# Relative attention with a routed expert gate: left sums by GpSimd in the window's first column, a block transpose on VectorE at a head's end, a slot table laid out by rows, output weights loaded early

## Chip, cores and metric

The kernel runs on one core of one Trainium2 chip. The metric is the device time of one execution in microseconds (us), median of several runs. A core has five engines that each work through their own instructions in order: TensorE (PE in the rows, with its weight loads as PEld), VectorE (DVE), ScalarE (ACT), GpSimd (POOL) and SyncE (SP, which here only issues DMAs). They wait for each other through semaphores.

## The reference

```python
xn = layernorm(x)                                  # x: (2, 2048, 256), f32
q, k, v = proj(Wq, bq), proj(Wk, bk), proj(Wv, bv)  # 16 heads of 16
idx = clip(arange(S)[None, :] - arange(S)[:, None], -128, 128) + 128
content  = einsum('bhqd,bhkd->bhqk', q, k)
relative = einsum('bhqd,qkd->bhqk', q, rel_k[idx])
w = softmax((content + relative) / sqrt(16))
s = (einsum('bhqk,bhkd->bhqd', w, v) + einsum('bhqk,qkd->bhqd', w, rel_v[idx])) @ Wo.T + bo
y = (gelu(xn @ W1[e]) @ W2[e])   # for each token the expert e = argmax(xn @ Wg + bg), 8 experts
x + s * silu(y)
```

The relative values `rel_v[idx]` are constant for all keys more than 128 to the left (`rel_v[0]`) and more than 128 to the right (`rel_v[256]`). Only in a window of 256 relative positions round the diagonal do they differ from key to key.

## The kernel before

It has three stages, each a block of its own with a barrier between: `project` (layernorm, q, k, v, gate logits, and the table arithmetic that gives every token a slot of its expert), `attend` (32 pairs of head and batch, called heads here), and `experts` (output projection, then 39 tiles of 128 slots through the experts).

`attend` is one software pipeline written out by hand. A head has 16 steps, one for each block of 128 queries or keys; each engine runs the same `step(hb, off)` over two heads at a time, and `Step(hb, off - k)` names the piece that lies k steps behind. In each step TensorE computes for the front (`a`) four pieces of 512 scores into two PSUM buffers `ps`, which VectorE reduces to row maxima (L1095, L1097); it may write a piece only when VectorE is done with the one before last (`s1_used`). For the back (`t`, 18 steps later) it computes the transposed scores `pst` again, which ScalarE exponentiates into `probs_T`. `turn_band` transposes the three blocks round the diagonal, whose probabilities are taken from `band` (the strip with relative scores), and `key_values` (`w`, 19 steps behind) adds values times probabilities into the PSUM accumulator `pout`: four blocks of 512 queries side by side, each in a group of 32 rows, of which row 16 is the sum of the probabilities. The first of them in a head waits until `pout` of the head before has been read (`out_evac`).

The values in `v_far` have the constant left or right relative value added. The diagonal block is counted as right, so two corrections follow. The window of 256 relative positions per query is written to HBM and read back sheared as `pwin` (128 queries x 4 blocks x 256), transposed by TensorE to `psmall`, copied by VectorE to `pwin_T`, and at the head's end `near_values` multiplies it with `rv_win` in two halves. Column 0 of the window is the relative position -128, where `rv_win` has a row of zeros. And the keys of the diagonal block that lie left of the query: GpSimd masks them out of `probs_T` into `left_T` (L847, once in each step), and `left_values` (L938) multiplies them with `rv_left`, the difference of the two constants.

After that ScalarE copies `pout` to `outT` (L1130), `turn_back` (L929) has TensorE transpose it in four pieces into `prel`, three steps later, and VectorE takes reciprocals (L1111) and multiplies (L1114) into `attn`. `prel` is also where TensorE puts the relative scores `q.rel_k` of every step (L1006), so the one after `turn_back` waits for `norm_done`.

GpSimd also does in every group of four steps: the ends and sides of `rel` (L880), the shift rows (L857 to L870, seven small operations chained by a semaphore), and copies to `q_back` (L837). At the start it fills the slot table `slot_tokens` (4992 slots, two int32 each) in HBM with `empty` (L900); in the last head it scatters the token numbers into it (L908, 32 indirect DMAs); SyncE then loads the table to SBUF as `slots` (L779), and only then does `attend` end.

`experts` begins with loads of `wo` and `bo`, then 16 MB of expert weights `w1` and `w2`. For each of 32 token tiles it gathers `attn`, transposes it, multiplies with `wo` and adds `bo` into `s_rows` (L1408), which GpSimd writes out to `x_and_s` in groups of four tiles, two buffers deep (L1279). Then come the slots: `turn_x`, `hidden`, `turn_hidden`, `output` (L1344) for 39 tiles.

## Time and profile before

| | us |
|---|---|
| median of 3 runs (2516.97 to 2523.92) | 2518.77 |
| the profiled execution | 2521.55 |
| its span | 2519.9 |
| TensorE busy | 2372.4 (94%) |
| VectorE busy | 1864.3 (74%) |
| ScalarE busy | 1685.1 (67%) |
| GpSimd busy | 1031.4 (41%) |

The span runs from the first to the last instruction; 1.65 us lie around it. Busy time leaves out waits. The three stages take about 158, 1989 and 373 us.

### The profile page before, as it was taken

The numbers are of one execution on the slowest core, as the hardware profiler recorded it, in microseconds if no ns is written. First come the engines' busy times: TensorE is split into PE (matmuls) and PEld (weight loads), VectorE is DVE, ScalarE is ACT, GpSimd is POOL, SyncE is SP. The second block draws the span as 40 slices with busy tenths as digits, with TensorE's granted clock in tenths as the row PEclk, the third lists the DMA queues.
The fourth block names the chain that finished last, engine by engine and source line by source line (L and its number), as shares of the span: only waits on it lengthen the run. The fifth ranks groups of instructions, "written<-read, shape, count | busy, mean of one in ns | idle before, by whom it ended". The sixth has DMA issues, their size and how long they took to land. (4 is left out here: it accounts for less than half of the span.)

```text
span 2519.9 us, 47614 instructions
## 1 busy us (share of the span) xinstructions
PE 2372.4 (94%) x14704; PEld 1176.4 (47%) x14704; DVE 1864.3 (74%) x5113; ACT 1685.1 (67%) x3898; POOL 1031.4 (41%) x2491
## 2 busy tenths in 40 slices
PE   6847999999999999999999999999999998799998
PEld 3411444444444444444444444444444443566666
DVE  6557888888888888888888888888888881333333
ACT  4522888888888888888778887888888876211121
POOL 1233444444444444444444444444444436133332
PEclk9965999999999999999999999999999999899999
DMA  5568898877778787878788778778877852922221
GB/s 165 168 157 239 266 284 267 247 253 232 245 246 254 233 250 248 252 244 251 248 253 245 242 248 251 239 239 249 249 241 245 247 169 52 346 75 68 67 64 50
DMA packets 351154, 540.98 MB, mean 215 GB/s; under 512 B 30608, under 2 KB 259392, under 8 KB 350912
## 3 DMA queue, kind: packets, MB, share of 16 engines
q1 hardware_dynamic: 336880, 502.76, 64.6%
q0 software_dynamic: 14032, 35.24, 4.7%
q8 instruction: 122, 2.00, 0.3%
q14 instruction: 120, 0.98, 0.1%
HBM read 272.60 MB, written 269.43 MB: 215 GB/s over the span
## 5 line engine op out<-in xcount | busy, mean ns | idle before, releaser
L1097 DVE TENSOR_REDUCE part<-ps 128x1 f32<-128x512 f32 (+3 forms) x2048 | 1197.5, 589 | 293.9 <-PE ps L984 280.1
L1153 ACT ACTIVATE probs_T<-pst 128x512 f32<-128x512 f32 (+3 forms) x2048 | 1019.6, 524 | 325.6 <-PE pst L993 319.2
L984 PE MATMUL ps<-k_front,q_front 96*128 96x512 bf16 x2048 | 803.9, 393 | 8.1 <-DVE part L1095 2.0
L933 PE MATMUL pout<-probs_T,v_far 128*32 128x512 f32 (+3 forms) x4864 | 546.0, 535 | 0.9 <-issue 0.9
L847 POOL TENSOR_TENSOR left_T<-probs_T,left_mask 128x128 f32<-128x128 f32 x512 | 217.5, 427 | 578.7 <-ACT probs_T L1136 429.6
L984 PEld LDWEIGHTS ps<-k_front,q_front 96*128 96x128 bf16 x2048 | 197.7, 97 | 436.3 <-DVE part L1097 236.9
L993 PE MATMUL pst<-q_back,k_left 102*128 102x512 bf16 (+3 forms) x1024 | 351.9, 344 | 2.4 <-ACT probs_T L1153 1.2
L993 PE MATMUL pst<-q_back,k_right 102*128 102x512 bf16 (+3 forms) x1024 | 350.1, 342 | 4.2 <-ACT probs_T L1153 3.0
L1166 ACT ACTIVATE band<-band,negm 128x384 f32<-128x384 f32 (+1 forms) x512 | 308.2, 602 | 2.2 <-POOL negm L870 2.2
L1095 DVE CUSTOM_DVE_ANT_0 band<-ps,band 128x256 f32<-128x256 f32 (+2 forms) x704 | 299.4, 425 | 0.0
L933 PEld LDWEIGHTS pout<-probs_T,v_far 128*32 128x32 f32 x4864 | 163.6, 108 | 242.5 <-issue 197.9
L1144 ACT ACTIVATE rel<-prel 128x257 f32<-128x257 f32 x512 | 203.3, 397 | 85.8 <-PE prel L1006 78.3
L1136 ACT ACTIVATE probs_T<-pband 128x384 f32<-128x384 f32 (+1 forms) x512 | 242.5, 474 | 21.7 <-PE pband L951 18.0
L951 PE MATMUL pband<-ident,band 128*128 128x128 f32 x1472 | 247.2, 274 | 0.0
L1077 DVE COPY pwin_T<-psmall 128x256 f32<-128x256 f32 x512 | 212.4, 415 | 45.0 <-PE psmall L1021 27.4
L880 POOL TENSOR_TENSOR rel<-rel,zero 128x1016 f32<-128x1016 f32 x128 | 240.6, 1880 | 0.0
L951 PEld LDWEIGHTS pband<-ident,band 128*128 128x128 f32 x1472 | 184.9, 141 | 99.5 <-issue 21.0
L1006 PE MATMUL prel<-rel_k,q_front 96*128 96x257 bf16 x512 | 144.7, 283 | 59.6 <-DMA q_front<-q_terms 28.7
L1021 PE MATMUL psmall<-ident,pwin 128*128 128x128 f32 x1024 | 198.3, 275 | 0.0
L1021 PEld LDWEIGHTS psmall<-ident,pwin 128*128 128x128 f32 x1024 | 135.5, 142 | 108.0 <-issue 26.5
L857 POOL TENSOR_TENSOR sh<-rel_ends,rmax 128x8 f32<-128x8 f32 x128 | 25.5, 199 | 381.1 <-DVE rmax L1060 370.0
L837 POOL COPY q_back<-shT 6x128 bf16<-6x128 bf16 x512 | 147.5, 288 | 49.0 <-POOL rel L880 14.4
(160 smaller groups left out, 2260.4 us busy)
## 6 DMA issues: line engine op xcount, KB each, us to landing
rel_scores<-rel SPq DMA_DIRECT2D x128, 1024.0 KB, 8.3
band_probs<-band SPq DMA_DIRECT2D x128, 768.0 KB, 4.0
pwin<-band_probs SPq DMA_DIRECT2D x128, 512.0 KB
band<-rel_scores SPq DMA_DIRECT2D x64, 768.0 KB, 6.6
band<-rel_scores SPq DMA_DIRECT2D x64, 576.0 KB, 5.4
w<-in_w_dram SPq DMA_DIRECT2D x16, 1024.0 KB, 16.9
band<-rel_scores SPq DMA_DIRECT2D x64, 128.0 KB, 5.8
q_terms<-terms SPq DMA_DIRECT2D x48, 128.0 KB
```

Source lines behind the costliest of these rows:

```text
L847: nc.gpsimd.tensor_tensor(left_T[:, w.s, :], own, left_mask[:, :], ALU.mult).then_inc(left_ready, 1)
L880: nc.gpsimd.tensor_tensor(sides, ends.unsqueeze(3).to_broadcast([P, CH, 2, M - 1]), zero_sides, ALU.add).then_inc(sides_done, 1)
L933: return nc.tensor.matmul(pout[32 * g:32 * g + 32, c0:c1], values, probs, start=first, stop=False, skip_group_check=True)
L951: mm = nc.tensor.transpose(pband[:, (i - t.s + 1) * P:(i - t.s + 2) * P], band[t.par][:, i, b * P:(b + 1) * P], con["ident"][:, :])
L984: nc.tensor.matmul(ps1[u % 2][:, :], q_front[a.par][:, a.s * P:(a.s + 1) * P], k_front[a.par][:, u * CW:(u + 1) * CW], start=True, stop=Tr ...
L993: mm = nc.tensor.matmul(pst[u % 2][:, c0:c1], k[:, t.s * P:(t.s + 1) * P], q_back[t.par][:, u * CW + c0:u * CW + c1], start=True, stop=True)
L1021: mm = nc.tensor.transpose(pnear[:, b * P:(b + 1) * P], pwin[t.r % 2][:, t.g, b * P:(b + 1) * P], con["ident"][:, :])
L1095: ins = nc.vector.tensor_tensor_reduce(dst, src, dst, 1.0, LOWEST, ALU.add, ALU.max, peak)
L1097: ins = nc.vector.tensor_reduce(peak, src, AX_X, ALU.max)
L1136: nc.scalar.activation(probs_T[t.s % 2][:, c0:c1], pband[:, c0 - b0:c1 - b0], ACT.Copy).then_inc(bandT_evac, 1)
L1153: ins = nc.scalar.activation(probs_T[t.s % 2][:, u * CW + c0:u * CW + c1], pst[u % 2][:, c0:c1], ACT.Exp, scale=SCALE)
L1166: nc.scalar.activation(band[y.par][:, y.s, c0:c1], band[y.par][:, y.s, c0:c1], ACT.Exp, bias=negm[y.par][:, y.s:y.s + 1], scale=SCALE).the ...
```

## The change

It does four things in `attend` and `experts`.

1. The left sum of a query (the sum of its masked diagonal probabilities) is now made by GpSimd from `band`, for four blocks at once: one multiplication with a mask over 128x4x128 numbers, six halvings by additions, and a last addition to `left_sum`. When the window `pwin` has landed, GpSimd copies the sums into its column 0, and `rv_win` gets the left difference in row 0. `left_T`, the mask over `probs_T` and `left_values` are gone, and TensorE waits for `left_set` where it waited for the window's DMA.
2. `finished` (ScalarE) and `turn_back` (TensorE) are gone. VectorE transposes `pout` in blocks of 32x32 straight into `turned`, in the step after the head's last, and takes reciprocals and products in the same step. `near_values` runs in both halves at once in the last quarter of the head's last step. Tokens of `attn` now lie in another order, and `experts` writes `s_rows` accordingly: 32 DMAs of a tile instead of 8 of four tiles, with four buffers of two tiles instead of two of four.
3. Slot s is now kept in row `(s % 128) * 39 + s // 128` of the table, so that a partition's 39 slots lie together. Five small VectorE operations in `project` compute this. The load of `slots` moves from SyncE at the end of `attend` to GpSimd at the start of `experts`.
4. `wo` and `bo` are loaded by SyncE early in `attend` and stay in SBUF.

```diff
-LAG_O = LAG_T + 5
+LAG_O = LAG_T + 2
...
                 link(v.tensor_reduce(posf[:, :], base[:, :, :], AX_X, ALU.add))
+                link(v.tensor_copy(pos_i[:, :], posf[:, :]))
+                link(v.tensor_scalar(row_i[:, :], pos_i[:, :], 7, None, ALU.logical_shift_right))
+                link(v.tensor_copy(rowf[:, :], row_i[:, :]))
+                link(v.tensor_scalar(posf[:, :], posf[:, :], float(XT), None, ALU.mult))
+                link(v.scalar_tensor_tensor(posf[:, :], rowf[:, :], 1.0 - P * XT, posf[:, :], ALU.mult, ALU.add))
...
+                    if hb == 2 and off == 2:
+                        sp.dma_start(wo[:, :, :], io["woT"].rearrange("(c p) n -> p c n", p=P)).then_inc(wo_in, 16)
+                        sp.dma_start(bo[:, :], io["bo"].partition_broadcast(P)).then_inc(wo_in, 16)
...
-                sp.wait_ge(slots_filled, 16 * TILES)
-                sp.dma_start(slots[:, :, :], dram["slots"].rearrange("(t p) k -> p t k", p=P)).then_inc(slots_in, 16)
...
+                    t = Step(hb, off - LAG_T)
+                    if t.g == 0 and t.valid:
+                        pool.wait_ge(win_in[t.r % 2], t.count(32, 16 * (t.r // 2 + 1)))
+                        pool.wait_ge(left_ready, t.count(4, t.r + 1))
+                        nc.gpsimd.tensor_copy(pwin[t.r % 2][:, :, 0], left_sum[:, t.r, :]).then_inc(left_set, 1)
+                    l = Step(hb, off - 8)
+                    if l.g == CH - 1 and l.valid:
+                        pool.wait_ge(band_ready, l.count(16, 4 * l.r + 4))
...
+                        nc.gpsimd.tensor_tensor(left[:, :, :], own, left_mask[:, :].unsqueeze(1).to_broadcast([P, CH, P]), ALU.mult).then_inc(left_link, 1)
+                        for h in range(6):
+                            n = P >> (h + 1)
+                            pool.wait_ge(left_link, k + h + 1)
+                            nc.gpsimd.tensor_tensor(left[:, :, 0:n], left[:, :, 0:n], left[:, :, n:2 * n], ALU.add).then_inc(left_link, 1)
+                        pool.wait_ge(left_link, k + 7)
+                        nc.gpsimd.tensor_tensor(left_sum[:, l.r, :], left[:, :, 0], left[:, :, 1], ALU.add).then_inc(left_ready, 1)
...
-                        nc.gpsimd.tensor_tensor(left_T[:, w.s, :], own, left_mask[:, :], ALU.mult).then_inc(left_ready, 1)
...
-                        pool.dma_start(dram["slots"].rearrange("(t p) k -> p t k", p=P), empty[:, :, :]).then_inc(slots_set, 16)
+                        pool.dma_start(dram["slots"].rearrange("(p t) k -> p t k", p=P), empty[:, :, :]).then_inc(slots_set, 16)
...
-                            pe.wait_ge(left_ready, ended.count(16, 16))
-                            left_values().then_inc(all_pv, 1)
...
-                            if t.s == LAG_O - LAG_T:
-                                wait(pe, norm_done, t.count(1, 0))
...
-                        if u >= 2 and w.s == NB - 1 and w.valid:
+                        if u == CH - 1 and w.s == NB - 1 and w.valid:
                             pe.wait_ge(winT_evac, w.count(16, 16))
-                            near_values(u - 2).then_inc(near_pv, 1)
-                        if u == 2 and o.s == NB - 1 and o.valid:
-                            turn_back()
+                            near_values(0)
+                            near_values(1).then_inc(all_pv, 1)
...
-                            pe.wait_ge(win_in[t.r % 2], t.count(32, 16 * (t.r // 2 + 1)))
+                            pe.wait_ge(left_set, t.count(4, t.r + 1))
...
+                    def turn_out():
+                        dve.wait_ge(all_pv, ended.count(1, 1))
+                        wait(dve, norm_done, ended.count(1, 0))
+                        nc.vector.transpose(turned[:, :, :].rearrange("p b v -> p (b v)"), pout[:, :]).then_inc(out_evac, 1)
...
-                        act.wait_ge(all_pv, ended.count(1, 1))
-                        nc.scalar.activation(outT, pout[:, :], ACT.Copy).then_inc(out_evac, 1)
...
-    SG = 4
+    SG, SR = 2, 4
...
-                sp.dma_start(wo[:, :, :], io["woT"].rearrange("(c p) n -> p c n", p=P)).then_inc(wo_in, 16)
-                sp.dma_start(bo[:, :], io["bo"].partition_broadcast(P)).then_inc(wo_in, 16)
...
+                pool.wait_ge(slots_filled, 16 * TILES)
+                pool.dma_start(slots[:, :, :], dram["slots"].rearrange("(p t) k -> p t k", p=P)).then_inc(slots_in, 16)
+                pool.wait_ge(slots_in, 16)
                 for T in range(RING):
                     fetch_x(T)
...
+                    for k in range(SG):
+                        t = SG * g + k
+                        pool.dma_start(s_tab[:, :, t // NB, t % NB, 1, :], s_rows[g % SR][:, k, :]).then_inc(s_out[g % SR], 16)
```

How this moves instructions is seen at two places. First TensorE at the end of a head, before: the first row is the last quarter of the head's last step, and `psmall`, `ps_0` after it begin the next step, in which the following head's first `pout<-probs_T,v_far` is the row that waits for `out_evac`.

```order
L933 MATMUL pout<-pwin_T,rv_win 32x512 [waits winT_evac]
L933 MATMUL pout<-pwin_T,rv_win 32x512 x3
L1021 MATMUL psmall<-ident,pwin 128x128 [waits winT_evac,win_in0]
L1021 MATMUL psmall<-ident,pwin 128x128
L984 MATMUL ps_0<-k_front,q_front 128x512 [waits s1_used]
L993 MATMUL pst<-q_back,k_left 128x128 [waits exp_done]
L933 MATMUL pout<-left_T,rv_left 32x512 [waits left_ready]
L933 MATMUL pout<-left_T,rv_left 32x512 x3
L1006 MATMUL prel<-rel_k,q_front 128x257 [waits r_evac]
L984 MATMUL ps_1<-k_front,q_front 128x512 [waits s1_used]
```

The same stretch of TensorE in the changed kernel, carried on to the row that waits for `out_evac`.

```order
L951 MATMUL pout<-pwin_T,rv_win 32x512 [waits winT_evac]
L951 MATMUL pout<-pwin_T,rv_win 32x512 x7
L1028 MATMUL psmall<-ident,pwin 128x128 [waits winT_evac,left_set]
L1028 MATMUL psmall<-ident,pwin 128x128
L997 MATMUL ps_0<-k_front,q_front 128x512 [waits s1_used]
L1006 MATMUL pst<-q_back,k_left 128x128 [waits exp_done]
L1014 MATMUL prel<-rel_k,q_front 128x257 [waits r_evac]
L997 MATMUL ps_1<-k_front,q_front 128x512 [waits s1_used]
L1006 MATMUL pst<-q_back,k_left 128x512 [waits exp_done]
L997 MATMUL ps_0<-k_front,q_front 128x512 [waits s1_used]
L1006 MATMUL pst<-q_back,k_left 128x512 [waits exp_done]
L951 MATMUL pout<-probs_T,v_far 32x128 [waits exp_done,bandT_evac,out_evac,v_built]
```

The four products with `rv_left` have gone from between the first scores of the step and `prel`, all eight window products stand together, and between them and the row that waits for `out_evac` only scores are left.

Second VectorE in the changed kernel, in that same next step (`ISA` is the fused addition and maximum over the diagonal blocks, with the read of its maximum).

```order
L1119 ISA band,part<-ps_0,band 128x256
L1119 ISA part 128x1
L1101 COPY pwin_T<-psmall 128x2x128 [waits all_pv,winT_mm]
L1077 STREAM_TRANSPOSE turned<-pout 128x512 [waits norm_done,all_pv]
L1121 TENSOR_REDUCE part<-ps_1 128x1 [waits s1_mm]
L1119 ISA band,part<-ps_1,band 128x128
L1119 ISA part 128x1
L1081 RECIPROCAL rden<-turned 128x16 [waits out_evac]
L1121 TENSOR_REDUCE part<-ps_0 128x1 [waits s1_mm]
L1085 TENSOR_TENSOR attn<-turned,rden 128x256 [waits den_ready]
L1121 TENSOR_REDUCE part<-ps_1 128x1 [waits s1_mm]
```

Before, the transpose was not there, ScalarE's copy stood in its place as the one that gives `out_evac`, and reciprocal and product came three steps later.

## Rows read from the trace of the kernel before

**Rows 1.** Stretch: its length, busy us of PE, PEld, DVE, ACT, POOL; clock, DMA share, GB/s.

```profile
325.30:2140.20 1814.90, 1787.08 (x12251) 821.05 (x12249) 1504.61 (x4225) 1458.69 (x3425) 812.28 (x2122) 1.00 0.77 239
```

**Rows 2.** Timeline of TensorE at one head's end: start, us, engine, line.

```profile
1140.85 0.38 PE L984 MATMUL ps<-k_front,q_front 96*128 96x512 bf16 x1
1141.22 1.06 PE L933 MATMUL pout<-left_T,rv_left 128*32 128x512 f32 x8
1142.21 0.28 PE L1006 MATMUL prel<-rel_k,q_front 96*128 96x257 bf16 x1
...
1143.30 1.06 PE L933 MATMUL pout<-probs_T,v_far 128*32 128x128 f32 x10
```

**Rows 3.** Timeline three steps later, TensorE alone.

```profile
1154.97 0.60 PE L929 MATMUL prel<-ident,pwin_T 128*128 128x128 f32 x4
1155.40 0.38 PE L984 MATMUL ps<-k_front,q_front 96*128 96x512 bf16 x1
...
1157.28 0.27 PE L1006 MATMUL prel<-rel_k,q_front 96*128 96x257 bf16 x1 [0.62 <-DVE attn L1114]
```

**Rows 4.** Who waited for whom, whole span: us, times, longest.

```profile
PE prel L1006 <- DVE attn L1114: 18.1, 29, 0.6
```

**Rows 5.** Timeline of VectorE and ScalarE at the head's end of Rows 2.

```profile
1141.27 0.42 DVE L1097 TENSOR_REDUCE part<-ps 128x1 f32<-128x256 f32 x1 [1.11 <-PE ps L984]
...
1141.95 0.42 DVE L1077 COPY pwin_T<-psmall 128x256 f32<-128x256 f32 x1
...
1142.35 0.60 ACT L1130 ACTIVATE pwin_T<-pout 128x512 f32<-128x512 f32 x1 [0.67 <-PE pout L933]
...
1145.10 1.28 DVE L1097 TENSOR_REDUCE part<-ps 128x1 f32<-128x512 f32 x2 [0.98 <-PE ps L984]
```

**Rows 6.** Groups of instructions by form: count, busy us, mean ns.

```profile
L1429 DVE COPY hT<-pt 128x512 f32<-128x512 f32 x78 | 53.9, 692 | 73.0 <-PE pt L1336 73.0
...
L1067 DVE STREAM_TRANSPOSE shT<-shb 128x128 bf16<-128x128 bf16 x128 | 38.7, 302 | 0.0
```

**Rows 7.** Groups on GpSimd, likewise; then its timeline in a later step.

```profile
L880 POOL TENSOR_TENSOR rel<-rel,zero 128x1016 f32<-128x1016 f32 x128 | 240.6, 1880 | 0.0
...
L862 POOL TENSOR_TENSOR sh<-sh,shb 128x8 f32<-128x8 f32 x128 | 25.8, 202 | 10.0
...
1154.50 0.43 POOL L847 TENSOR_TENSOR left_T<-probs_T,left_mask 128x128 f32<-128x128 f32 x1
...
1163.45 0.20 POOL L857 TENSOR_TENSOR sh<-rel_ends,rmax 128x8 f32<-128x8 f32 x1 [2.57 <-DVE rmax L1060]
```

**Rows 8.** DMA issues (last figure: us to landing), and TensorE's longest wait in `attend`.

```profile
slot_tokens<-empty POOLq DMA_DIRECT2D x1, 39.0 KB, 23.0
...
201.84 0.39 PE L1006 MATMUL prel<-rel_k,q_front 96*128 96x257 bf16 x1 [14.81 <-DMA q_front<-q_terms]
```

**Rows 9.** Timeline from the end of `attend` into `experts`; last row: DMA share, GB/s.

```profile
2140.54 0.42 DVE L1114 TENSOR_TENSOR attn<-prel,rden 128x256 f32<-128x256 f32 x1
...
2148.16 10.22 SPq L1250 DMA_DIRECT2D w<-in_w_dram  x8
...
2150.31 0.95 POOL L1259 DMA_INDIRECT xs<-x_norm,slots  x1 [0.30 <-issue]
...
2152.06 0.29 DVE L1401 COPY at<-attn 128x256 f32<-128x256 f32 x1 [4.51 <-DMA bo<-in_bo_dram]
...
2158.71 0.82 POOL L1279 DMA_DIRECT2D x_and_s<-s_rows  x1 [7.45 <-DVE s_rows L1408]
...
2166.55 0.42 DVE L1408 TENSOR_TENSOR s_rows<-ph,bo 128x256 f32<-128x256 f32 x1 [3.61 <-DMA x_and_s<-s_rows]
...
2196.72 0.42 DVE L1408 TENSOR_TENSOR s_rows<-ph,bo 128x256 f32<-128x256 f32 x1 [0.44 <-PE ph L1305]
...
2207.39 3.62 PE L1344 MATMUL py<-w,hT 128*128 x16
...
2204.00:2206.00 2.00, 1.00 0.43 153
```

More of the change, by code:

```diff
@@ L822, in step @@
                             wait(pool, st_mm, q.count(64, -64))
[L824 to L826 removed]
+                        window = Step(hb, off - LAG_T)
+                        if window.valid:
+                            pool.wait_ge(left_set, window.count(4, window.r + 1))
+                        sums = Step(hb, off - 11)
+                        if sums.valid:
+                            pool.wait_ge(left_ready, sums.count(4, sums.r + 1))
                         sides = Step(hb, off + LAG_R - 4)
@@ L919, in step @@
                     w = Step(hb, off - LAG_T - 1)
-                    o = Step(hb, off - LAG_O)
-                    ended = Step(hb, off - LAG_T - 2)
-                    def turn_back():
-                        pe.wait_ge(out_evac, o.count(1, 1))
-                        wait(pe, norm_done, o.count(1, 0))
-                        wait(pe, r_evac, x.count(16, x.s + 1) if x.valid else NBH * 16)
-                        for r in range(CH):
-                            mm = nc.tensor.transpose(prel[:, r * P:(r + 1) * P], pwin_T[:, 0, S - CW + r * P:S - CW + (r + 1) * P], con["ident"][:, :])
-                        mm.then_inc(back_mm, 1)
+                    ended = Step(hb, off - LAG_O)
                     def weighted(g, c0, c1, values, probs, first=False):
                         return nc.tensor.matmul(pout[32 * g:32 * g + 32, c0:c1], values, probs, start=first, stop=False, skip_group_check=True)
-                    def left_values():
-                        for g in range(CH):
-                            mm = weighted(g, 0, CW, rv_left[:, :], left_T[:, CH * g:CH * g + CH, :].rearrange("p i c -> p (i c)"))
-                        return mm
                     def near_values(b):
@@ L1104, in step @@
                             maxima[u]()
-                    o = Step(hb, off - LAG_O)
-                    if o.s == NB - 1 and o.valid:
-                        back = prel[:, :].rearrange("p (r g d) -> p r g d", r=CH, g=CH)
-                        rv = rden[:, :].rearrange("p (r g) -> p r g", r=CH)
-                        dve.wait_ge(back_mm, o.count(1, 1))
-                        nc.vector.reciprocal(rv, back[:, :, :, HD]).then_inc(den_ready, 1)
-                        dve.wait_ge(den_ready, o.count(1, 1))
-                        dst = attn[:, o.n, :, :].rearrange("p (g r) d -> p r g d", g=CH)
-                        nc.vector.tensor_tensor(dst, back[:, :, :, 0:HD], rv.unsqueeze(3).to_broadcast([P, CH, CH, HD]), ALU.mult).then_inc(norm_done, 1)
+                        if ended.s == NB - 1 and ended.valid and u < 3:
+                            finish[u]()
                 loop(step)
@@ L1120, in step @@
                 def step(hb, off):
-                    ended = Step(hb, off - LAG_T - 2)
                     x = Step(hb, off + LAG_R)
@@ L1147, in step @@
                         wait(act, pv_done, t.count(16, t.s - 1))
-                        wait(act, left_ready, t.count(16, t.s - 1))
                     for u in range(CH):
@@ L1169, in _, with experts @@
                 loop(step)
-def experts(nc, io, dram, con, attn, expert_i, slots, out):
-    SG = 4
+def experts(nc, io, dram, con, attn, expert_i, slots_filled, slots, wo, bo, out):
+    SG, SR = 2, 4
     with ExitStack() as ctx:
@@ L1189, in experts @@
         w2 = sb("w2", [P, NE, FC, D], F32)
-        wo = sb("wo", [P, DC, D], F32)
-        bo = sb("bo", [P, D], F32)
         at = two("at", [P, D], F32)
         aT = two("aT", [P, DC, P], F32)
-        s_rows = two("s_rows", [P, SG, D], F32)
+        s_rows = [sb(f"s_rows{i}", [P, SG, D], F32) for i in range(SR)]
         xs = ring("xs", [P, D], F32)
@@ L1212, in experts @@
         s_ready = sem("s_ready")
-        s_out = [sem(f"s_out{i}") for i in range(2)]
+        s_out = [sem(f"s_out{i}") for i in range(SR)]
         w1_in = sem("w1_in")
@@ L1477, in build @@
         slots = sb("slots", [P, XT, 2], I32)
-        attend(nc, io, dram, con, pos_i, slots, attn)
-        experts(nc, io, dram, con, attn, expert_i, slots, out)
+        wo = sb("wo", [P, DC, D], F32)
+        bo = sb("bo", [P, D], F32)
+        slots_filled = ctx.enter_context(nc.semaphore("slots_filled"))
+        attend(nc, io, dram, con, pos_i, slots_filled, wo, bo, attn)
+        experts(nc, io, dram, con, attn, expert_i, slots_filled, slots, wo, bo, out)
 _INS = ["x", "wqT", "wkT", "wvT", "wg", "bq", "bk", "bv", "bg", "rel_kT", "rel_v", "woT", "bo", "w1", "w2"]
```

81 lines of the change are left out of this document (39 added, 42 removed).

## The prediction

> **What bounds the kernel now.** I read the busy times by stretch first. Over the 31 head periods between the first and the last head's reciprocal, 1814.9 us or 58.5 us a head, TensorE is busy 98.5% of the time at the full granted clock, VectorE 82.9%, ScalarE 80.4%, GpSimd 44.8% [rows 1]. So `attend` is bound by TensorE, and what is taken from its queue comes off the end, as long as VectorE, which it feeds through two PSUM buffers, keeps pace. Then the timeline of one head's end. Overlapping durations there mislead: what an instruction costs TensorE is the distance between starts. The four products with `rv_left` start at 1141.22 and the next at 1142.21: 0.99 us, 1.07 with the gap of 0.08 ahead of them that a change to `pout` costs (I count every such gap so) [rows 2]. The four transposes of `turn_back` take 0.43 us, from 1154.97 to 1155.40, and the `prel` behind them waits 0.62 us for VectorE's product [rows 3]; the list of waits has this as 18.1 us in 29 waits [rows 4]. It is the one wait of TensorE that comes back in every head.
>
> Outside that rhythm two stretches stand out. At 187 us TensorE stops for 14.8 us, waiting for the front operands of the second head, while the DMA that fills the slot table is in flight for 23.0 us, 39 KB in pieces of 8 bytes [rows 8]. And between the last product into `attn` (ends 2140.96) and the third gather of `experts` (2152.06) lie 11.1 us: the table load, the barrier, then `bo` [rows 9].
>
> **The loop over heads.** Removed: 1.07 (left products), 0.43 (turn back), 0.62 (the wait), and one gap of 0.08, since the window products now stand together. That makes 2.2 us a head if nothing takes their place.
>
> Something does. Before, the first `key_values` of the next head started at 1143.30, 2.45 us behind the step's first scores (1140.85) [rows 2]. Without the left products it could start at 1.4. But it waits for `out_evac`, which now comes from VectorE, behind a reduction, the fused addition and the window's copy. VectorE began that step at 1141.27, 0.42 behind the scores, and reached the window's copy at 1141.95; the copy ends at 1142.37 [rows 5]. The block transpose of `pout` behind it has no row: 128x512 in f32 from PSUM. Its nearest rows are a copy of 128x512 f32 from PSUM (692 ns) and the same operation on 128x128 in bf16 (302 ns) [rows 6]. As a pure stream like the copy it takes 0.70; if the 302 ns scaled with elements alone it would be 1.2, and with bytes too 2.4. Below, it is twice as wide as the window's copy of 128x256 in 0.42 [rows 5], so hardly under 0.5. I take 0.70, for the rows of 128 columns lie close to a stream as well. Counted by full durations the transpose ends at 1143.07, and with 0.05 for the semaphore `key_values` starts at 1143.1; successive VectorE instructions overlap by 0.07 (the copy starts 0.68 behind a pair whose durations sum to more) and TensorE starts the step some 0.1 earlier for the gap saved, so 1142.8 on the old scale. Gain at this place: 0.5 of the 1.07, of which the rest is a new TensorE wait of some 0.4 before `key_values` and one of some 0.3 for the step's first reduction.
>
> VectorE has to carry the transpose, the reciprocal and the product more in this step, where it idled 1.11 us ahead of 1141.27 and 0.98 ahead of 1145.10 [rows 5]; the last two it gives back three steps later. Its load goes from 48.5 to 49.2 us a head against some 57: enough. At the turn-back place the full 1.05 comes off, as nothing there has been waiting on VectorE but this. **Sum: 0.5 + 1.05 = 1.55 us a head, 48 us in 31 periods.** Bounds: 2.2 a head (68 us) with no new wait; with a transpose of 1.2 us it is 1.05 a head (33 us); with 2.4 us, -0.15 a head (-5 us).
>
> The rule of the Trainium skill here, from "Vector Engine (DVE) Microarchitecture Reference", section 3.8, is that the reorder array in front of VectorE transposes 32x32 blocks while sustaining one element per cycle per lane. With the 0.96 GHz of "VectorE: DVE Perf Modes", Specifications, 384 columns more than the bf16 row are 0.40 us more, an estimate of 0.70 for the transpose; by it the ends at 1.2 and 2.4 would fall away. No row before shows a 4-byte transpose.
>
> **GpSimd.** Removed: 512 masks of 427 ns, all off the path. Added: 128 times eight operations over 1020 numbers a partition. One operation over 1016 numbers takes 1880 ns, a small one 202 ns, and a chained one idles 10.0/128 = 0.08 us [rows 7]: 1.88 + 7 x 0.20 + 7 x 0.08 = 3.8 us, +0.2 for the copy into the window. Behind it on GpSimd stands the shift chain. The chunk can begin where the first mask of the group stood, at 1154.50, and ends at 1158.3; the shift chain starts at 1163.45 when the row maxima come [rows 7]. 5.1 us to spare, so it costs nothing; without that cover each us more would reach the back's operands, which have their own lead of a step and more. In a group of four steps (14.2 us) GpSimd then works some 9.5. If small strided operations took 0.43 each, as a full mask does, the chunk would be 5.3 us and still fit. TensorE now waits for a copy queued on GpSimd instead of the DMA; the copy stands at the head of GpSimd's step, and the window's transposes at the end of TensorE's, so I count nothing for it. ScalarE only loses work.
>
> **The start.** With rows of 312 bytes the table's fill is 128 pieces instead of 4992, so it no longer holds up the DMAs around it. The second head's operands should then land about when they are wanted. I take 13 of the 14.8 us; upper end 14.8, lower end 6, if the megabyte transfers in flight beside them are themselves the delay. Against it: five small VectorE operations in a chain on the path to `attend`, at the 0.20 that a small one takes on GpSimd [rows 7] some 1.1 us, and 0.2 for the extra `rv_win` operation. Net 11.7.
>
> **The seam.** Ahead of it 1.4 us fall away: 1.07 of left products, ScalarE's copy (0.60), the turn back, for a transpose. The barrier no longer waits for the table, so the weights start not at 2148.16 but some 0.8 behind the product's end at 2139.5: 2140.3. Their transfer ran at full DMA rate up to about 2205 (153 GB/s is left in the window from 2204) [rows 9]; 57 us later gives 2197. The first `py` stood at 2207.39 and comes 10.2 us behind the projection, which ended at 2197.15. The projection now begins 11 us earlier, but GpSimd must load the table (0.8 to issue like an `s_rows` DMA, some 4 to land, my estimate: half of an `s_rows` DMA's 7.8) and issue three gathers (1.25 apiece) before the first `s_rows` goes out, at 2149 instead of 2158.71 [rows 9]. Eight tiles fit in the buffers and wait; the ninth, which stood at 2166.55, comes at 2149 + 0.8 + 7.0 = 2157. The 24 tiles from it on took 30.6 us in bursts of eight, each waiting for a DMA; buffers of two tiles let go a little earlier, but there are four times the DMAs to issue, so I leave 30.6. The projection ends at 2187.5, `py` follows at about 2198, by this path as by the weights. **Gain 9.4**; bounds 4 (small DMAs behind the weights take 12 us, not 8) and 12. The 39 tiles behind it are unchanged.
>
> **Sum.** 48 + 11.7 + 9.4 = 69 us. Against the profiled execution's own time, 2521.55, that is 2452.4; the median of the runs shown lies 2.8 lower, so 2450.
>
> **Rivals.**
> - *VectorE's turn becomes the bound.* The transpose or the reductions behind it take a microsecond of TensorE at each head's end. For it: VectorE's queue at that point has no slack once the left products no longer cover it, and there are only two `ps` buffers. Against: it idles about 1 us per step there. Time: the loop gives 0.3 to 1 us a head, 10 to 31, with 21 from start and seam: 2466 to 2488. Chance 0.17.
> - *Slower: the transpose goes far above its rows.* It has one place, `out_evac`, and costs TensorE 31 x (T - 0.70). The loop's gain is gone at T = 2.25 us and all of the 69 at T = 2.9; at 4 us the kernel takes 2552. The bf16 row speaks against it, even at four times the elements and twice the bytes (2.4 us). Chance 0.04.
> - *The changes of the two seams do nothing*, because the large transfers and not the table hold up the second head's operands, and the projection, late behind GpSimd's loads, sets `py` as before. Then 48 - 1.3 + 1.4 = 48 remain: 2471. Against: the table's 39 KB were in flight for 23.0 us, which nothing else there explains. Chance 0.07.
> - *No change to be told* (within 0.3%): half of the first and all of the third at once. 0.03.
> - The forecast, all terms in their bounds: 0.69.
>
> **Numbers.** A measurement of this kernel tells 0.3% (7.5 us) from no change. The range runs from full gains (68 + 13 + 8, 2430) to a loop with half its gain and a start at its lower end (24 + 5 + 7.5, about 2482). Faster 0.92, same 0.04, slower 0.04.
>
> **What the profile after would show.** `STREAM_TRANSPOSE turned<-pout` near 700 ns; TensorE's waits on it some 0.4 us, 31 times; head period 57.0 us instead of 58.5; eight GpSimd operations in 3.8 us with idle time left ahead of `sh`; no wait of 14.8 us near 187 us; first weights' DMA within 1 us of the last product; `py` some 58 us behind it. The prediction is wrong if the transpose is above 1.2 us, if VectorE's reductions make TensorE wait through the steps after a head's end, or if the second head's operands still land 15 us late.

## The result, and the profile after

| | median us | runs |
|---|---|---|
| before, on the same chip | 2518.54 | 2516.97 to 2523.92 |
| changed kernel | 2449.41 | 2448.36 to 2451.22 |

The ratio is 0.9723, 95% interval 0.9706 to 0.9739: 69 us less. The profiled execution took 2450.3 us, its span is 2448.7, 71.2 below the span of before.

The busy times of the whole span come first (page, parts 1 and 5; in part 5 the columns are busy us, mean ns, idle before and its releaser), with one of the new groups on GpSimd and the place where GpSimd idles.

```profile
PE 2317.8 (95%) x14320; PEld 1162.7 (47%) x14320; DVE 1878.5 (77%) x5150; ACT 1655.4 (68%) x3866; POOL 1319.1 (54%) x3155
...
L847 POOL TENSOR_TENSOR left<-left 128x256 f32<-128x256 f32 (+5 forms) x768 | 279.5, 364 | 60.2
...
L885 POOL TENSOR_TENSOR sh<-rel_ends,rmax 128x8 f32<-128x8 f32 x128 | 25.5, 200 | 493.8 <-DVE rmax L1067 493.8
```

The bound has not changed. Over the head periods between the first and the last block transpose of the shift chain (`shT`), TensorE is busy 98.6% (windows of the changed kernel, columns as in [rows 1]; the first row is a stretch of `project`, which matters below).

```profile
100.00:120.00 20.00, 16.73 (x55) 8.79 (x53) 12.48 (x28) 13.79 (x26) 3.58 (x6) 1.00 0.67 186
197.50:2015.20 1817.70, 1791.68 (x12084) 828.17 (x12083) 1607.48 (x4510) 1461.92 (x3473) 1093.84 (x2840) 0.99 0.81 253
```

The new operations on VectorE (instructions of one tile: ns minimum, median, maximum, and first and last start in us).

```profile
L1077 DVE STREAM_TRANSPOSE turned<-pout x32: 704/706/717, 295.2 to 2071.8; 128x512 f32<-128x512 f32 x32
L1081 DVE RECIPROCAL rden<-turned x32: 247/249/255, 296.4 to 2072.6; 128x16 f32<-128x16 f32 x32
```

One head's end, TensorE and VectorE together (timeline), the counterpart of [rows 2] and [rows 5].

```profile
1101.15 0.44 PE L1028 MATMUL psmall<-ident,pwin 128*128 128x128 f32 x2
1101.43 0.38 PE L997 MATMUL ps<-k_front,q_front 96*128 96x512 bf16 x1
...
1101.85 0.42 DVE L1121 TENSOR_REDUCE part<-ps 128x1 f32<-128x256 f32 x1 [1.97 <-PE ps L997]
...
1102.53 0.42 DVE L1101 COPY pwin_T<-psmall 128x256 f32<-128x256 f32 x1
...
1102.67 0.39 PE L997 MATMUL ps<-k_front,q_front 96*128 96x512 bf16 x1 [0.26 <-DVE part L1119]
1102.87 0.70 DVE L1077 STREAM_TRANSPOSE turned<-pout 128x512 f32<-128x512 f32 x1
...
1103.67 1.07 PE L951 MATMUL pout<-probs_T,v_far 128*32 128x128 f32 x10 [0.39 <-issue]
```

VectorE gets its first scores, reduces them, copies the window and then transposes. The third `ps` waits 0.26 us for the first reduction, and `key_values` (the `pout` row) starts 0.10 us behind the transpose's end (1102.87 + 0.70). That its wait of 0.39, labelled "issue", is for `out_evac` is what runs 3 and 5 below show. The list of waits has it once for nearly every head (us, times, longest).

```profile
PE pout L951 <- issue: 11.8, 30, 0.4
```

**Where the 71.2 us of span lie.** Five marks are in both traces: the first issue of `q_front`, the first and the last `shT`, the last window product (its weight load), the first `py`. 30 of the heads' ends lie between the second and the third mark and one lies behind them; the forecast's 31 x 1.55 us are split in that way.

| stretch | before | after | difference | forecast |
|---|---|---|---|---|
| start to first `q_front` | 158.4 | 154.0 | -4.5 | +1.1 |
| to the first `shT` | 54.9 | 43.5 | -11.4 | -12.8 |
| 127 groups of four steps | 1867.1 | 1817.8 | -49.4 | -46.5 (30 x 1.55) |
| to the last window product | 56.5 | 55.5 | -1.0 | -1.5 (1 x 1.55) |
| to the first `py` | 70.4 | 63.6 | -6.8 | -9.4 |
| to the end | 312.6 | 314.3 | +1.8 | 0 |

The loop came out at 49.4 / 30 = 1.65 us for each head's end. To see in which steps, I took the distance between the starts of successive window transposes (`psmall`), one pair a step, on TensorE:

| step | before | after |
|---|---|---|
| with the window products | 5.66 | 5.42 |
| first of the next head | 4.55 | 4.34 |
| second, third | 3.47, 3.44 | 3.48, 3.43 |
| fourth (turn back before) | 3.81 | 3.38 |
| fifth (wait for the product before) | 4.13 | 3.35 |

In this pair of heads that is 0.24 + 0.21 at the head's end and 0.43 + 0.78 at the turn-back place, 1.66 in all. The other heads agree: a full period, from the first window transpose of one head to that of the next, is 59.37 us before and 57.69 after in each head from the second to the last but one. The wait that [rows 3] print as 0.62 cost 0.78: the step grew by that. A printed idle time starts at the modelled end of the matmul before (1156.28 + 0.38), while the next matmul would have started 0.22 behind that one's start.

**The start and the seam.** The table's fill lands in 1.8 us rather than 23.0 (DMA issues):

```profile
slot_tokens<-empty POOLq DMA_DIRECT2D x1, 39.0 KB, 1.8
```

and the second head's front operands hold TensorE up for 3.2 us rather than 14.8 (timeline of TensorE).

```profile
185.98 0.40 PE L1014 MATMUL prel<-rel_k,q_front 96*128 96x257 bf16 x1 [3.21 <-DMA q_front<-q_terms]
```

What the table's fill did to the loads beside it stands in the 20 us from the issue of these operands on, in the kernel before and then in the changed one (columns as in [rows 1]): the DMA engines were busy all through in both, but moved 129 GB/s beside the old fill and 284 without it.

```profile
181.00:201.00 20.00, 5.37 (x11) 0.89 (x10) 6.31 (x15) 0.97 (x3) 2.03 (x2) 0.50 1.11 129
```

```profile
176.60:196.60 20.00, 14.88 (x30) 2.59 (x29) 15.81 (x42) 3.94 (x8) 4.10 (x11) 0.50 0.96 284
```

The five new operations on VectorE take 1.1 us, from the start of the first to the start of the conversion that alone stood there before (timeline of VectorE).

```profile
151.06 0.18 DVE L411 CAST pos_i<-posf 128x32 int32<-128x32 f32 x1
...
152.16 0.18 DVE L416 CAST pos_i<-posf 128x32 int32<-128x32 f32 x1
```

Past the last product into `attn` (2072.87 to 2073.29), the timeline of SyncE's queue, GpSimd and TensorE reads as follows.

```profile
2073.89 7.08 SPq L1253 DMA_DIRECT2D w<-in_w_dram  x8
...
2074.04 0.59 POOL L1278 DMA_DIRECT2D slots<-slot_tokens  x1 [7.99 <-POOLq L699]
2079.54 1.01 POOL L1262 DMA_INDIRECT xs<-x_norm,slots  x1 [4.92 <-DMA slots<-slot_tokens]
...
2083.06 5.56 POOL L1288 DMA_DIRECT2D x_and_s<-s_rows  x8
...
2134.33 5.40 PE L1352 MATMUL py<-w,hT 128*128 x16 [2.38 <-DMA w<-in_w_dram]
```

The weights start 0.6 us behind the last product, and `py` comes 60.4 us behind them instead of the forecast 58, now waiting for the weights themselves. The last +1.8 us is one `py` at a lower clock: 5.40 us against 3.62 in [rows 9]. The granted clock from 2134 to 2140 was 0.72, and 1.00 from 2207 to 2213 before.

### The profile page after: what moved, and what is told of

Read it like the earlier page. It is cut to its first block and busy times, and to the rows that moved or that the text cites. A ratio compares the mean times of both kernels' runs of the same rounds, so it can differ in the third digit from the quotient of the medians.

```text
span 2448.7 us, 47775 instructions
## 1 busy us (share of the span) xinstructions
PE 2317.8 (95%) x14320; PEld 1162.7 (47%) x14320; DVE 1878.5 (77%) x5150; ACT 1655.4 (68%) x3866; POOL 1319.1 (54%) x3155
## 5 line engine op out<-in xcount | busy, mean ns | idle before, releaser
L951 PE MATMUL pout<-probs_T,v_far 128*32 128x512 f32 (+3 forms) x4864 | 546.1, 535 | 12.8 <-issue 11.8
L847 POOL TENSOR_TENSOR left<-left 128x256 f32<-128x256 f32 (+5 forms) x768 | 279.5, 364 | 60.2
```

Source lines behind the costliest of these rows:

```text
L847: nc.gpsimd.tensor_tensor(left[:, :, 0:n], left[:, :, 0:n], left[:, :, n:2 * n], ALU.add).then_inc(left_link, 1)
L951: return nc.tensor.matmul(pout[32 * g:32 * g + 32, c0:c1], values, probs, start=first, stop=False, skip_group_check=True)
```

## Experiments

| run | change | median us | ratio to before, 95% |
|---|---|---|---|
| e1_table_rows | before + table by rows | 2499.80 | 0.9907 to 0.9941 |
| e8_rows_by_tile | e1 + one DMA a tile | 2504.26 | 0.9929 to 0.9963 |
| e4_left_products | after, left products back | 2455.29 | 0.9735 to 0.9768 |
| e3_turn_twice | after, transpose twice | 2467.33 | 0.9780 to 0.9813 |
| e5_chunk_twice | after, chunk twice | 2481.68 | 0.9834 to 0.9867 |
| e6_table_columns | after, table by columns | 2461.25 | 0.9753 to 0.9785 |
| e7_weights_late | after, `wo`, `bo` late | 2450.78 | 0.9713 to 0.9745 |
| e2_turn_first | after, transpose ahead of window copy | 2439.35 | 0.9666 to 0.9698 |
| e9_turn_ahead | e2, transpose ahead of reductions | 2425.50 | 0.9615 to 0.9643 |
| e10_rows_by_scalar | e9, ScalarE issues `s_rows` | 2453.65 | 0.9727 to 0.9758 |

The kernel before had medians of 2517.7 to 2519.6 us beside them.

**1. The table by rows alone (e1_table_rows).** The kernel before, with the five new VectorE operations on `posf` and

```diff
-  sp.dma_start(slots[:, :, :], dram["slots"].rearrange("(t p) k -> p t k", p=P))
+  sp.dma_start(slots[:, :, :], dram["slots"].rearrange("(p t) k -> p t k", p=P))
```

and the same for the fill; SyncE still loads the table at the end of `attend`.

> The kernel before with one part of the change alone: the slot table by rows (the five VectorE operations, and both table DMAs in pieces of 312 bytes), the load still on SyncE. Theory (the fill's 4992 pieces hold up the DMAs beside them): the second head's operands land early, TensorE's wait near 187 us falls from 14.8 to 3 us as in the changed kernel, and the table's load at the end of attend gets a little shorter: 11 to 14 us less, 2505 to 2508 us. Rival (the megabyte transfers hold them up, the rest of the 71 us came from elsewhere): 2518 to 2520 us, the wait still near 15 us.

It gained 19.8 us, more than expected (17.6 in the spans of the two traces). The wait near 187 us fell to 3.2 us, and from the first `q_front` to the first `shT` it took 43.4 us (54.9 before, 43.5 in the changed kernel), so the whole gain in this stretch is the table's. Most of the rest is at the seam: the table's load lands in 1.9 us instead of 5.3, the weights start 1.5 us behind the end of the last product instead of 7.2, and the stretch from the last window product to `py` is 65.8 us, 4.7 less than before. The loop stayed (1866.4).

**2. The table by columns in the changed kernel (e6_table_columns).** The reverse edit.

> The changed kernel with the slot table laid out by columns as before (pieces of 8 bytes), five small VectorE operations fewer; the table's load stays on GpSimd behind the last product. Theory: the table's fill is in flight for some 20 us again and holds up the second head's operands: about 12 us more in the wait near 187 us; and the table's load, 4992 pieces beside the weights, lands later than the 5.2 us of the changed kernel, which makes the gathers and the first output DMAs late by some us, part of it on the path: 2461 to 2469 us. Rival, the start's gain came from something else (the clock in the project stage): 2448 to 2452 us.

2461.3 us, 11.8 more than the changed kernel. The fill is in flight for 23.6 us again and the start takes 55.5 us from `q_front` to the first `shT`; the load at the seam lands in 11.4 us, not 5.2 (DMA issues).

```profile
slot_tokens<-empty POOLq DMA_DIRECT2D x1, 39.0 KB, 23.6
...
slots<-slot_tokens POOLq DMA_DIRECT2D x1, 39.0 KB, 11.4
```

The wait of the second head's front operands is back (timeline of TensorE).

```profile
203.28 0.40 PE L1009 MATMUL prel<-rel_k,q_front 96*128 96x257 bf16 x1 [15.37 <-DMA q_front<-q_terms]
```

From the last window product to `py` it is 66.7 us against 63.6. Done and undone, the layout moves the stretch from the first `q_front` on by 11.5 and 12.0 us; the five operations lie ahead of it. The rival (another origin of the gain) falls.

**3. The transpose twice (e3_turn_twice).** A first transpose of `pout` into a spare tile ahead of the one that gives `out_evac`.

```diff
+  nc.vector.transpose(turned2[:, :, :].rearrange("p b v -> p (b v)"), pout[:, :])
   nc.vector.transpose(turned[:, :, :].rearrange("p b v -> p (b v)"), pout[:, :]).then_inc(out_evac, 1)
```

> The changed kernel with the transpose of pout done twice (the first into a spare tile). Theory (no slack at that place): each head pays the distance of two starts, 0.6 us, 31 times: 19 us more, 2468 us. Rival (VectorE idles a microsecond in that step and absorbs it): under 5 us more, 2454 us at most.

17.9 us more, 0.58 us for each of the 31 heads' ends. The first step of a head takes 4.94 us rather than 4.34; no other step changed. The wait ahead of `key_values` grew by 18.0 us (list of waits; 11.8 in the changed kernel).

```profile
PE pout L952 <- issue: 29.8, 30, 1.0
```

The transpose's whole duration, less the overlap with its neighbour, stands on TensorE's path.

**4. The left products again (e4_left_products).** The changed kernel with GpSimd's masks of `probs_T`, `rv_left` and the four products back, the chunk and the copy into the window gone; the turn stays on VectorE.

```diff
+                        if u == 0 and ended.s == NB - 1 and ended.valid:
+                            pe.wait_ge(left_ready, ended.count(16, 16))
+                            left_values().then_inc(all_pv, 1)
```

> The changed kernel with the left sums as before: GpSimd masks probs_T into left_T once a step, and TensorE multiplies it with rv_left at the head's end; all else as changed. Theory (the wait for the transpose has taken the left products' place, so taking them out won little): all_pv comes some 0.1 to 0.2 us later and TensorE fills its former wait with the products; key_values starts 0.2 us later, 6 us more than the changed kernel, 2455 us. Rival (savings add up, each 1.07 us of TensorE counts in full): 33 us more, 2482 us.

5.9 us more. The first step of a head takes 4.54 us rather than 4.34, the step ahead of it stays at 5.42. So the products' 1.07 us are worth only 0.20: without them TensorE waits for the transpose instead. With them its list of waits has none ahead of `key_values`, and 2.3 us instead of 9.6 for VectorE's fused addition. The 0.24 us of the step ahead is not theirs; this run keeps the window products together, and with them that gain, but no run parts the two halves again by itself.

**5. The transpose one place earlier (e2_turn_first).** In VectorE's step, between the first reduction and the window's copy.

```diff
+                        if u == 0 and ended.s == NB - 1 and ended.valid:
+                            turn_out()
                         if u == 0 and w.valid:
                             window()
```

> The changed kernel with VectorE's transpose of pout ahead of the window's copy instead of behind it. Theory (TensorE's wait before the next head's first values hangs on the end of that transpose): key_values starts 0.34 us earlier in each head and the wait of 0.39 us nearly goes, 31 x 0.3 = 9 us less than the changed kernel, 2440 us. Rival (VectorE's whole queue in the step is what binds, so its order is all one): 2448 to 2451 us.

2439.4 us, 10.1 less. The first step of a head takes 4.01 us instead of 4.34, as the copy's 0.34 is out of `key_values`' way. The 11.8 us of waits ahead of `key_values` are gone from the list.

**6. Two places earlier (e9_turn_ahead).** The transpose at the head of VectorE's step, and `key_values` of a head's first step back behind the second scores.

```diff
-                        if u == (2 if w.s == 0 else 1) and w.valid:
+                        if u == 1 and w.valid:
                             key_values()
...
+                    if ended.s == NB - 1 and ended.valid:
+                        turn_out()
```

> The kernel of the second experiment (2439.4 us) with the block transpose one place earlier still, at the head of VectorE's step, where VectorE idles 1.97 us for the step's first scores, and key_values of a head's first step back at its usual place behind the second scores. Theory: the 0.25 us that TensorE still waits for the step's first reduction is there because its 1.0 us of key_values no longer stands ahead of the third scores; with both moved the reduction is hidden, and the transpose ends 0.1 us ahead of key_values: 31 x 0.25 = 8 us less, 2431 to 2433. Rival, the transpose now stands ahead of the reductions and TensorE waits for it, or for the reductions behind it, as long as before: 2438 to 2446.

2425.5 us: 13.9 less than e2, 23.9 less than the changed kernel, 92 less than before. The gain is larger than expected. The timeline of the head's end shows no wait left on TensorE; the list of waits has 4.0 us for `part` in the whole span where the changed kernel had 11.6.

```profile
1091.36 0.44 PE L1028 MATMUL psmall<-ident,pwin 128*128 128x128 f32 x2
1091.50 0.72 DVE L1077 STREAM_TRANSPOSE turned<-pout 128x512 f32<-128x512 f32 x1 [1.41 <-PE pout L951]
...
1092.55 1.06 PE L951 MATMUL pout<-probs_T,v_far 128*32 128x128 f32 x10
1093.55 0.39 PE L997 MATMUL ps<-k_front,q_front 96*128 96x512 bf16 x1
...
1094.77 0.38 PE L1028 MATMUL psmall<-ident,pwin 128*128 128x128 f32 x2
```

The step takes 3.41 us (1091.36 to 1094.77), 0.60 less than in e2, and the one behind it 3.64 instead of 3.50. That is 0.46 net, 14.3 over 31 heads' ends, where I had priced the named wait of 0.25 alone. The transpose now runs in the 1.4 to 2.0 us in which VectorE idled anyway, and `key_values` covers the reductions. The run moved both at once and does not tell what each gives alone.

**7. GpSimd's chunk twice (e5_chunk_twice).** The mask and the halving additions a first time into a spare tile, ahead of the real ones.

> The changed kernel, with GpSimd's chunk (mask and seven halving additions) done twice for each group of four steps; the first result goes to a spare tile. Added: 4.2 us on GpSimd in each of 128 groups (14.3 us apart). Theory, the chunk is covered: GpSimd idles 3.86 us ahead of the shift copies in each group, so 0.3 us of a group is uncovered and most of that is taken by the lead of the back's operands: 2449 to 2456 us, and the idle time ahead of the shift copies falls from 493.8 us to under 100. Rival, GpSimd is on the path already through the copy into the window's first column (TensorE waits for it at a step's end): several us for each group's delay, over 2459 us.

2481.7 us, 32.3 more: the theory fell. The mean of 3.86 us of idle time a group is not the slack. In the timeline of the changed kernel the four groups of a head idle 3.4, 2.0, 3.7 and 6.3 us ahead of `sh`, and in the second of them GpSimd also builds `v_far`.

```profile
1064.91 0.20 POOL L885 TENSOR_TENSOR sh<-rel_ends,rmax 128x8 f32<-128x8 f32 x1 [3.35 <-DVE rmax L1067]
1078.57 0.20 POOL L885 TENSOR_TENSOR sh<-rel_ends,rmax 128x8 f32<-128x8 f32 x1 [1.98 <-DVE rmax L1067]
1092.52 0.20 POOL L885 TENSOR_TENSOR sh<-rel_ends,rmax 128x8 f32<-128x8 f32 x1 [3.71 <-DVE rmax L1067]
1109.03 0.20 POOL L885 TENSOR_TENSOR sh<-rel_ends,rmax 128x8 f32<-128x8 f32 x1 [6.26 <-DVE rmax L1067]
```

With 4.2 us more in each, three groups in a row run late: in this run's timeline GpSimd does not idle ahead of `sh` from 1068.56 to 1126.86. TensorE meets the delay in the step with the window products, the first that reads the next head's `q_back`, whose last part needs the shift rows of the fourth group (timeline of TensorE).

```profile
1116.83 0.38 PE L1015 MATMUL pst<-q_back,k_left 102*128 102x512 bf16 x1 [0.46 <-POOL q_back L882]
```

The list of waits has both of GpSimd's (us, times, longest).

```profile
PE pst L1015 <- POOL q_back L882: 14.9, 30, 0.9
...
PE psmall L1037 <- POOL pwin L834: 6.0, 1, 6.0
```

That step takes 6.03 us rather than 5.42. The copy into the window, the rival's place, shows once (6.0 us) and not again, so the rival named the right order of size and the wrong place. The shift chain accounts for 0.61 x 31 = 19 us. The one wait and the step behind it, 1.5 us longer, make 7.7. The remaining 6 us lie in the first head, from its first `shT` to the end of its first step with `psmall` (5.9 us longer): there VectorE's `shT` waits for GpSimd (list of waits, 195 to 250 us; the changed kernel has no such wait there).

```profile
DVE shT L1102 <- POOL shb L826: 3.6, 2, 1.9
```

**8. Output weights late (e7_weights_late).** `wo` and `bo` loaded by SyncE ahead of the expert weights, as before.

> The changed kernel with the output weights and their bias loaded by SyncE at the seam, ahead of the expert weights, as before. Theory: the projection starts some 4.5 us later and the expert weights some 1 to 2 us later; as the latter set the first py, the kernel takes 1 to 3 us more, 2450.5 to 2452.5. Rival, the projection's start decides through its own chain (s_rows, gathers, py): 4.5 us more, 2454.

2450.8 us, in the theory's range but also within the spread of the changed kernel. The stretch to `py` is 67.2 us instead of 63.6, 3.6 more, but the `py` of the changed kernel then lost 1.8 us to its lower clock in the profiled execution. By the medians the early load is worth 1.4 us, which these runs do not tell from nothing; what the 3.6 us of the traces are worth in other executions is open.

**9. One DMA for each tile of `s_rows` (e8_rows_by_tile).** On e1, to find why the weights became slower.

```diff
-  pool.dma_start(s_tab[:, SG * g:SG * (g + 1), 1, :], s_rows[g % 2][:, :, :])
+  for k in range(SG):
+      pool.dma_start(s_tab[:, SG * g + k, 1, :], s_rows[g % 2][:, k, :])
```

> The kernel before with the slot table by rows (the first experiment: 2499.8 us) and, in place of one DMA for four tiles of s_rows, one DMA for each tile, at the same addresses with the same bytes. Theory, more DMAs cost the DMA engines time of their own: some 3,300 more packets under 512 bytes, the rate in the middle of the projection falls from 409 and 389 to some 370 GB/s, and the expert weights end some 60 us behind their start and not 57; py was not waiting for them there, so the time is 2499.5 to 2502. Rival, it is the scattered addresses of the changed kernel's token order that slow its weights: packets and rate stay as in the first experiment, time 2499.8.

The theory fell: the count of DMAs costs nothing that shows in the rate. Two windows of the projection, in e8, then in the changed kernel (last columns: DMA share, GB/s).

```profile
2142.00:2162.00 20.00, 14.79 (x76) 12.05 (x75) 7.83 (x26) 4.98 (x13) 6.46 (x12) 0.95 1.04 410
2162.00:2177.00 15.00, 13.27 (x68) 10.73 (x67) 6.58 (x21) 4.22 (x11) 6.41 (x12) 0.95 1.08 389
```

```profile
2086.00:2106.00 20.00, 13.04 (x61) 10.39 (x60) 6.06 (x20) 3.83 (x10) 8.12 (x13) 0.83 1.05 374
2106.00:2121.00 15.00, 14.53 (x78) 11.62 (x76) 7.52 (x24) 5.79 (x13) 9.65 (x14) 1.00 1.11 369
```

The rate is that of e1 (409 and 389) with a DMA for each tile, and is lower in the changed kernel, which differs from e8 in the token order, but also in the buffers and the place of `wo` and `bo`. GpSimd's packets differ too (page, part 3: packets, MB, share), e8 first.

```profile
q0 software_dynamic: 14352, 35.24, 4.6%
```

```profile
q0 software_dynamic: 17456, 35.33, 4.9%
```

With 32 DMAs and the same bytes of `s_rows` in both, the changed kernel's queue carries 3104 packets and 0.09 MB more. By the sizes of the packets in the trace, the table's load, which e8 has in SyncE's queue, is 32 packets and 0.04 MB of that; the other 3072 are 96 for each DMA, of 16 bytes each. Packets and rate do not go strictly together: e7, with the same packets as the changed kernel, moved 393 and 363 GB/s in the two windows. An issue takes GpSimd 688 ns rather than 540. A tile is now four runs of 32 tokens, for the block transpose leaves tokens in blocks of 32 (`s_tab` in four dimensions). The median of e8, above the ranges of both sides, lies 4.5 us above e1's, with intervals that overlap; their profiled spans are 2501.5 and 2502.3, so I draw nothing from it.

**10. ScalarE issues the DMAs (e10_rows_by_scalar).** As e9, with `put_rows(t - 3)` on ScalarE behind each `turn_attn(t)`.

> As the run before, and ScalarE instead of GpSimd issues the 32 DMAs of s_rows. Theory: the transfers of the changed kernel in GpSimd's queue carry some 3,000 small packets that the order by columns of 128 tokens does not have, and slow the expert weights from 410 to 374 GB/s; from ScalarE's queue they go without, the weights end some 57 us behind their start rather than 60, and py comes 1 to 2.5 us sooner: 1 to 2.5 us less than the run before. Rival, the small packets come from the address pattern whatever the queue, and the issuing costs ScalarE, which stands in the projection's chain, 32 x 0.05 to 0.5 us: 0 to 10 us more.

2453.7 us, 28 more than e9: both sides missed the size. The timeline of the two queues at the projection's start:

```profile
2060.17 20.38 SPq L1257 DMA_DIRECT2D w<-in_w_dram  x3
2060.61 0.51 ACTq L1385 DMA_DIRECT2D x_and_s<-s_rows  x1
2061.70 4.85 ACTq L1385 DMA_DIRECT2D x_and_s<-s_rows  x1
2066.68 5.91 ACTq L1385 DMA_DIRECT2D x_and_s<-s_rows  x1
```

An issue takes ScalarE 2.2 us in the median and up to 5.9 while the weights are being issued, and from the last product into `attn` to the last `s_rows` it takes 80 us instead of 49. In the packets the theory had a point: ScalarE's queue carries 4224 for the 32 DMAs, none of them of 16 bytes, and GpSimd's loses 4608. What they cost the weights this run can't tell, as the projection beside them is so much slower.

## Why the prediction was right

The forecast, all terms in their bounds, is what came: 2449.4 against 2450. That the two are within 1 us is partly luck: the loop gave 2.4 us more than its term (50.4 for 48), the start behind `q_front` and the seam 1.4 and 2.6 less, and a few us of the measured gain are a difference between executions (see the start). By its own steps:

- **The transpose** took 0.706 us against 0.70, the row of the copy; the ends at 1.2 and 2.4 us fall away. The trace agrees with the rule of the Trainium skill, "Vector Engine (DVE) Microarchitecture Reference", section 3.8 (a block transpose keeps up one element per cycle and lane): the estimate worked out from it was 0.70.
- **The head's end** gave 0.45 against 0.5. The new waits are there as described: 0.26 for the first reduction, 0.39 ahead of `key_values`. But the split differs: the products' removal gave 0.20 (run 4), standing together 0.24, where I had counted 0.08 for the gap.
- **The turn-back place** gave 1.21 against 1.05 in the pair of heads measured, since the printed wait of 0.62 was 0.78 of TensorE's time. Together the steps gave 1.66 a head against 1.55. The 58.5 us a head that the forecast read from [rows 1] is a mean with the shorter last head in it; a full period was 59.37 and is now 57.69.
- **GpSimd.** The chunk takes 1.28 + 2.18 + 0.20 + 7 x 0.08 = 4.2 us against 3.8; I had priced the eight operations like one over 1016 numbers and seven small ones, 3.28, and they take 3.66. It cost nothing, as forecast (TensorE's waits name nothing of GpSimd's), but of "5.1 us to spare" the tightest group of a head had 2.0 left afterwards; run 7 shows the price beyond that.
- **The start** gave 11.4 of the 12.8 forecast from `q_front` on, and the five operations took the 1.1 us of their term. Yet `project` was 4.5 us shorter. No run shows the change as the reason: the changed kernel and e2 have the same instructions up to there and reach `q_front` at 154.0 and 158.3 us, e1 and e8 likewise at 157.7 and 155.6. The granted clock goes with a part of it: over 100 to 120 us it was 0.83 in the traces of before, e1 and e6 (158.4, 157.7 and 159.3 us), that is, at 1.2 GHz for a third of the stretch and at 2.4 otherwise; 1.00 in the changed kernel, e3, e4, e7 and e8 (152.9 to 155.6); and 0.91 in e2, e5, e9 and e10 (155.3 to 158.3). The profiled executions with a late `q_front` are also long ones: those of before, e1, e2 and e6 lie 3.0 to 7.3 us above the median of their kernel (that of e10 1.8), the changed kernel's 0.9. So the medians hold some 2.4 of these 4.5 us (4.5 less the 2.1 between 3.0 and 0.9, my estimate).
- **The seam** gave 6.8 of 9.4, the term with the largest error. The first `s_rows` DMA started at 2083.06, 9.8 us behind the product's end (9.5 forecast) and the projection ended at 2121.5, 48.2 behind it (48.0 forecast). What failed is "57 us later" for the weights: they took 60, at 374 and 369 GB/s instead of 410 and 389, and `py` waited 2.4 us for them. Of the seam's gain, 4.7 us is the table's (run 1); the early output weights' part is 1.4 by the medians and 3.6 by one pair of traces, and neither is clear of the spread (run 8).
- **The rivals.** "VectorE's turn becomes the bound" has a true core: all that TensorE still waits for at a head's end is VectorE's order, 0.77 us a head net, which runs 5 and 6 together gave back. It was a price already in the sum, not one on top. The slower rival's slope holds: in run 3 each further transpose of 0.71 us cost 0.58 to 0.60 of TensorE's time.

## What to carry to other kernels

When work leaves the bound engine, look at what its time was covering: here 1.07 us of products gave 0.20, because a transpose queued behind a reduction and a copy came next; moved to a place where its engine idled, with the products that need it moved up to cover the reductions, the same transpose left no wait on TensorE and 24 us came back. Price a wait on a pipelined engine by the distance between starts of the whole step, before and after, not by the idle time printed. Judge the cover of an off-path engine by its tightest group and what accumulates up to it, not by the mean idle time.

## What the runs showed of the hardware

- A block transpose of 128x512 f32 from PSUM takes VectorE 706 ns, about the 692 of a copy of that size [rows 6].
- One DMA of 39 KB in 4992 pieces of 8 bytes is in flight for 23.0 and 23.6 us (before, e6) and holds up loads beside it: the DMA engines were busy all through but moved 129 GB/s. In 128 pieces it lands in 1.8 us (changed kernel, e1), and beside it they moved 284 and 287.
- An issue of a DMA by ScalarE took from 0.5 to 5.9 us (e10) while SyncE was issuing megabyte loads (the second eight 4.0 to 12.0 us each); GpSimd's issues of the same DMAs took 0.69 to 0.84 (e9).
- A DMA that writes a 128-row tile as four runs of 32 rows carried 96 packets of 16 bytes more in GpSimd's queue than one that writes it in one run (changed kernel, e8), and none of 16 bytes in ScalarE's (e10). The large loads beside it ran at 374 rather than 410 GB/s; that the packets are the cause was not tested by itself.
